# Layer 0: half mean on another engine, tile rounds in another order, virtual-row matmul first in its bank

## The reference

```
# layer 0
g  = groupnorm(x)                        # 8 groups of 2 channels, over H and W
Y  = conv3x3(rfft2(g)) + bias            # complex 3x3 convolution in the frequency domain
x1 = x + irfft2(Y)
# layer 1
out = x1 + mean15x15(groupnorm(x1))      # box mean with zero padding
```

## Time and profile before

| what | value |
|---|---|
| median of 3 runs | 4614.39 us (4611.82 to 4618.62) |
| profiled execution | 4609.17 us, span 4607.4 us |
| PE busy | 4004.6 us, 87% |
| DVE busy | 3595.1 us, 78% |
| POOL busy | 2617.5 us, 57% |
| ACT busy | 2369.4 us, 51% |

### The profile page before, as it was taken

One profiled execution on the slowest core, in us unless ns is written; L12 is line 12 of the kernel. 1 busy time (PEld: TensorE's weight loads), 2 busy tenths in 40 slices (PEclk: granted clock), 3 DMA queues, 4 the chain that ended last, 5 costly groups with the idle time before them and its releaser, 6 DMA issues.

```text
span 4607.4 us, 120149 instructions
## 1 busy us (share of the span) xinstructions
PE 4004.6 (87%) x40080; PEld 2607.0 (57%) x40080; DVE 3595.1 (78%) x6413; ACT 2369.4 (51%) x3744; POOL 2617.5 (57%) x2177
## 2 busy tenths in 40 slices
PE   5299898998989989899898998899988998989988
PEld 1155564556645566455655556555565555655557
DVE  7798875987769877698767987679865888659986
ACT  0177523775247742477315773167722776227752
POOL 4087652875437754477535775267742777418765
PEclk9699998999999999899999999999999999999999
DMA  7311173111731127211371114611155111641114
GB/s 167 119 47 44 40 203 98 46 46 54 205 81 46 46 79 200 60 46 46 98 204 39 44 46 129 176 37 46 38 154 151 42 46 33 177 129 46 46 36 138
DMA packets 221883, 406.04 MB, mean 88 GB/s; under 512 B 96049, under 2 KB 171169, under 8 KB 205217
## 3 DMA queue, kind: packets, MB, share of 16 engines
q1 hardware_dynamic: 221600, 402.52, 32.1%
HBM read 255.55 MB, written 146.80 MB: 87 GB/s over the span
## 4 chain that ended last, share of the span: by engine, by line
PE 45%; DVE 25%; issue 16%; ACT 7%; DMA 3%; DVEq 3%; POOL 1%; SPq 1%; ACTq 1%; POOLq 0%
PE h_ps L609 13%; PE p L535 10%; PE p L462 9%; PE p L635 5%; DVE ob_all L1031 5%; DVE ob_all L1037 4%; DVE img L1046 4%; DVE stat L1049 4%; ACT arena L714 3%; PE h_ps L535 3%; DMA img<-in_x 2%; ACT arena L700 2%; PE h_ps L428 1%; PE p L435 1%; DVE ob_all L893 1%
## 5 line engine op out<-in xcount | busy, mean ns | idle before, releaser
L535 PE MATMUL p<-arena,bd_all 64*64 64x512 f16 x16896 | 1311.5, 380 | 171.6 <-DVE ob_all L1037 88.6
L1165 POOL TENSOR_TENSOR arena<-arena 128x512 f16<-128x512 f32 x512 | 591.7, 1156 | 878.4 <-ACT arena L700 799.4
L535 PEld LDWEIGHTS p<-arena,bd_all 64*64 64x64 f16 x16896 | 611.5, 105 | 642.1 <-issue 491.6
L1223 POOL TENSOR_TENSOR arena<-img 128x512 f32<-128x512 f32 x392 | 497.1, 1269 | 588.0 <-PE h_ps L609 559.5
L428 PE MATMUL h_ps<-hilbert,arena 128*128 128x256 f16 (+1 forms) x6240 | 788.1, 276 | 29.8 <-DVE arena L1004 25.1
L680 ACT ACTIVATE arena<-h_ps 128x512 f16<-128x512 f32 x512 | 305.7, 597 | 965.4 <-PE h_ps L609 732.3
L699 ACT ACTIVATE arena<-img,sc 128x512 f16 (+1 forms) x512 | 439.4, 858 | 625.2 <-PE p L579 419.4
L428 PEld LDWEIGHTS h_ps<-hilbert,arena 128*128 128x128 f16 (+1 forms) x6240 | 614.0, 99 | 171.1 <-issue 35.6
L1174 POOL TENSOR_TENSOR ob_all<-ob_all,img 128x512 f32<-128x512 f32 x512 | 658.6, 1286 | 82.9 <-POOL ob_all L1172 72.8
L1172 POOL TENSOR_TENSOR ob_all<-ob_all 128x512 f32<-128x512 f32 x512 | 656.1, 1281 | 31.1 <-DVE ob_all L1037 31.1
L462 PE MATMUL p<-img,bd_all 128*48 128x512 f32 x1024 | 530.6, 627 | 115.9 <-DMA img<-in_x 79.4
(11 more groups left out here) (154 smaller groups left out, 4561.8 us busy)
## 6 DMA issues: line engine op xcount, KB each, us to landing
img<-in_x SPq DMA_DIRECT2D x256, 512.0 KB, 6.9
out<-ob_all SPq DMA_DIRECT2D x512, 256.0 KB, 3.1
bd_all<-bd_dram SPq DMA_DIRECT2D x512, 192.0 KB, 2.2
wrap_mat<-tab_wrap_h SPq DMA_DIRECT2D x512, 32.0 KB, 2.0
bd_dram<-ob_all SPq DMA_DIRECT2D x16, 768.0 KB, 3.5
arena<-tab_hilbert_kernel SPq DMA_DIRECT2D x8, 256.0 KB, 3.3
hilbert<-tab_hilbert SPq DMA_DIRECT2D x1, 522.0 KB, 3.9
cosw<-tab_cosw SPq DMA_DIRECT2D x1, 320.0 KB, 2.8
```

The source lines that it names most:

```text
L535: m = mm(bank[out_half * HP:(out_half + 1) * HP, :], low(half, 6 * lm + (j if own else j + 1)), (g_part if own else h_part)(half, lp), sta ...
L1165: G.tensor_tensor(gp[s][:, 1, :], g32, gp[s][:, 0, :], ALU.subtract).then_inc(g_split, 1)
```

## The change

Three things are done, all in layer 0:

1. The half mean of a row (two columns) is no longer a DVE instruction in `finish_row`, but two POOL instructions in a new function `mean_half`, called in POOL's slot t for row t-3 after `add_terms` and before the running sum, and for the last three rows after the last `add_terms`.
2. The tile rounds of `mix` fill the base, sine and cosine banks in that order (it was cosine, base, sine). The two waits for DVE's terms stand before round 1 and round 3 (they stood before round 0 and round 1).
3. The virtual-row matmul, which closed the base bank, now opens it, ahead of these waits; in the first row of an image its wait for the virtual row moves with it. What waited for `p0_ready` of a finished row to reuse buffers (ACT twice, SP) now waits for `p2_ready`, which is counted by the last round.

```diff
-                        sp.wait_ge(p0_ready, b * T + i * NG + (PRIMED + s - NG + 1))
+                        sp.wait_ge(p2_ready, b * T + i * NG + (s - NG + 1))
...
-                    pe.wait_ge(t1_done, PRIMED + n)
-                    pe.sem_inc(mix_step, 1)
-                    first_half = [(p1[:], 2)] * 3 + [(p0[s], 0)] * 3 + [(p2[:], 4)] * 3
+                    if first == 0 and s == 0:
+                        pe.wait_ge(v_wrap, b + 1)
+                    if first > 0:
+                        pe.wait_ge(x1_done, PRIMED + n - (NG - 1))
+                    mm(p0[s], wrap_mat[s][:], wrap_row[:], start=True, stop=False, skip_group_check=True)
+                    first_half = [(p0[s], 0)] * 3 + [(p2[:], 4)] * 3 + [(p1[:], 2)] * 3
                     for r in range(10):
                         if r == 1:
+                            pe.wait_ge(t1_done, PRIMED + n)
+                            pe.sem_inc(mix_step, 1)
+                        if r == 3:
                             pe.wait_ge(t2_done, PRIMED + n)
-                            pe.sem_inc(mix_step, 1)
-                        if r == 3 and first > 0:
-                            pe.wait_ge(x1_done, PRIMED + n - (NG - 1))
                             pe.sem_inc(mix_step, 1)
...
-                    if first == 0 and s == 0:
-                        pe.wait_ge(v_wrap, b + 1)
-                    mm(p0[s], wrap_mat[s][:], wrap_row[:], start=False, stop=True, skip_group_check=True).then_inc(p0_ready, 1)
+                    m.then_inc(p2_ready, 1)
...
-                        act.wait_ge(p0_ready, PRIMED + n - (NG - 1))
+                        act.wait_ge(p2_ready, n - (NG - 1))
...
-                        act.wait_ge(p0_ready, PRIMED + n - 1)
+                        act.wait_ge(p2_ready, n - 1)
...
                     V.bn_stats(stat[:, t, :], img[:, t, :]).then_inc(x1_counted, 1)
-                    if first * NG + s >= NG:
-                        dve.wait_ge(x1_whole, n - (NG - 1))
-                    dve.wait_ge(x1_counted, n + 1)
-                    V.scalar_tensor_tensor(half_row[:, s, :], stat[:, t, 1:6:3], -0.5, known[:, t, :],
-                                           ALU.mult, ALU.add).then_inc(half_made, 1)
...
+                def mean_half(n, t, s, first):
+
+                    if first * NG + s >= NG:
+                        pool.wait_ge(x1_whole, n - (NG - 1))
+                    pool.wait_ge(x1_counted, n + 1)
+                    G.tensor_tensor(half_row[:, s, :], stat[:, t, 1:6:3], minus_half[:], ALU.mult).then_inc(half_scaled, 1)
+                    pool.wait_ge(half_scaled, n + 1)
+                    G.tensor_tensor(half_row[:, s, :], half_row[:, s, :], known[:, t, :],
+                                    ALU.add).then_inc(half_made, 1)
...
                     if t >= 1:
                         add_terms(n - 1, i * NG + s - 1, (s - 1) % NG, first - (s < 1))
+                    if t >= 3:
+                        mean_half(n - 3, i * NG + s - 3, (s + 1) % NG, first - (s < 3))
                     if sum_t is not None:
                         presum(b * T + sum_t, sum_t)
...
                 add_terms(b * T + T - 1, T - 1, (T - 1) % NG, T // NG)
+                for t in range(T - 3, T):
+                    mean_half(b * T + t, t, t % NG, T // NG)
```

More of the change, by code:

```diff
@@ L202, in build @@
         half_row = sb("half_row", [P, NG, 2])
+        minus_half = sb("minus_half", [P, 2])
         vmean = sb("vmean", [NV, 2])
@@ L249, in build @@
                                                       sem("x1_done"))
-        x1_counted, half_made, x1_whole, stat_fixed = (sem("x1_counted"), sem("half_made"), sem("x1_whole"),
-                                                       sem("stat_fixed"))
+        x1_counted, half_scaled, half_made, x1_whole, stat_fixed = (sem("x1_counted"), sem("half_scaled"),
+                                                                    sem("half_made"), sem("x1_whole"),
+                                                                    sem("stat_fixed"))
         bias_in, bias_added = sem("bias_in"), sem("bias_added")
@@ L554, in mix @@
                             if r == 6:
-                                pe.wait_ge(p2_half, n + 1)
+                                pe.wait_ge(p1_half, n + 1)
                                 pe.sem_inc(mix_step, 1)
-                            m = half_terms(bank, j, r % 3, 0, r < 6, r >= 6)
+                            m = half_terms(bank, j, r % 3, 0, 3 <= r < 6, r >= 6)
                             if r == 2:
-                                m.then_inc(p1_half, 1)
+                                m.then_inc(p0_half, 1)
                             if r == 5:
-                                m.then_inc(p0_half, 1)
+                                m.then_inc(p2_half, 1)
                             if r == 8:
-                                m.then_inc(p2_ready, 1)
+                                m.then_inc(p1_ready, 1)
                         if r >= 1:
@@ L566, in mix @@
                             if r == 4:
-                                pe.wait_ge(p1_half, n + 1)
+                                pe.wait_ge(p0_half, n + 1)
                                 pe.sem_inc(mix_step, 1)
                             if r == 7:
-                                pe.wait_ge(p0_half, n + 1)
+                                pe.wait_ge(p2_half, n + 1)
                                 pe.sem_inc(mix_step, 1)
@@ L573, in mix @@
                             if r == 3:
-                                m.then_inc(p2_half, 1)
+                                m.then_inc(p1_half, 1)
                             if r == 6:
-                                m.then_inc(p1_ready, 1)
-                    if first == 0 and s == 0:
-                        pe.wait_ge(v_wrap, b + 1)
-                    mm(p0[s], wrap_mat[s][:], wrap_row[:], start=False, stop=True, skip_group_check=True).then_inc(p0_ready, 1)
+                                m.then_inc(p0_ready, 1)
+                    m.then_inc(p2_ready, 1)
                 front(0, 0, 0)
@@ L814, in _ @@
             V.memset(sc[:, 24:25], 1.0 / HB)
+            V.memset(minus_half[:], -0.5)
             V.memset(flat[:, 0:4 * 144], 0.0)
@@ L1077, in layer0 @@
                     finish_row(b * T + t, t, t % NG, T // NG)
-                dve.wait_ge(half_made, (b + 1) * T)
+                dve.wait_ge(x1_counted, (b + 1) * T)
+                dve.wait_ge(half_scaled, (b + 1) * T)
                 V.scalar_tensor_tensor(parity_mean, parity_mean, 0.5, known[:], ALU.mult, ALU.add).then_inc(stat_fixed, 1)
```

## The result

The changed kernel takes 5531.6 us (4 runs, 5529.1 to 5533.1) against 4613.1 us for the kernel before beside it: ratio 1.1988, 95% interval 1.1967 to 1.2009. The forecast was 5508 us. Of all executions in this document one was disturbed, one of the six of e9 (5089.0 us at a granted clock of 0.743), and it is in no ratio. The profiled execution went from 4609.2 to 5533.1 us, its span from 4607.4 to 5531.3.

The account below looks back on a forecast made before the run. It took DVE, the fuller partner of TensorE, to bound the kernel before, and a 7.09 us ACT-POOL circle the changed one. Circle +910 and tail -16 us on 4614.4 us gave 5508 us, range 5350 to 5760.

Parts of the forecast that it names:

- The circle of ACT and POOL: Layer 0 rows: normalise, POOL's slot, half mean and ACT's add wait in a ring, 7.09 us a row, +910 us; 83%.
- The total: Whole kernel: +910 and -16 us make +894 us on the median 4614.4 us, giving 5508 us.
- The small operations: POOL's two 128x2 half-mean instructions: 160 ns each, low end -100 us, high end +320 us in all.
- The estimate of 0.31 us: POOL's half-mean operations priced from the skill page's dispatch figure: sum 137 us higher, 5645 us.
- The start of an image: Row 0's rounds wait for the virtual row, 1.0 us later per image, won back by later rows: net nothing.
- The tail: End of layer 0: last half mean 2 us earlier per image, POOL's last presums covered: -16 us for 8 images.
- What bounds the kernel before: Layer 0 rows: DVE and TensorE hand the row to each other, DVE fuller; slack on ACT and POOL.
- a gain that counts only if nothing else is slower: New tile-round order: TensorE could go at its floor, ACT and SP wait about 0.2 us less.
- Rival 3: Layer 0 rows: no circle, DVE's relief shows and TensorE's floor of 4.45 us decides: -271 us, 4343 us; 3%.
- The clock: TensorE in steady rows drops to 1.2 GHz, likelier 8.2 us a row, 6055 us; 4%.

Follow-up runs that it names:

- e9: The kernel of e6, but in each image's first row the virtual-row matmul and its wait close the base bank as in the kernel before: 4393.0 us, ratio 0.9517.
- e3: The changed kernel, but ACT adds the half mean to row t-4 in slot t instead of t-3: 4410.7 us, ratio 0.9559.
- e4: The changed kernel, but POOL makes the half mean at the start of its slot, ahead of split_g: 4405.9 us, ratio 0.9552.
- e7: The changed kernel with two more, unused 128x2 operations on POOL ahead of the half mean: 5667.6 us, ratio 1.229.
- e8: The changed kernel with the virtual-row matmul given five times instead of once: 5535.7 us, ratio 1.2004.
- e10: The changed kernel, but each image's first row closes its base bank with the virtual-row matmul and its wait as before: 5515.3 us, ratio 1.1947.
- e2: The kernel before with only the half mean moved to POOL, rounds and virtual-row matmul as before: 5514.7 us, ratio 1.1959.
- e5: The kernel before, half mean still on DVE but as two one-column instructions with one SBUF tensor and a per-partition scalar: 4517.4 us, ratio 0.9792.
- e6: The half mean of e5 on DVE together with the changed round order and the virtual-row matmul in front: 4401.8 us, ratio 0.9545.

## Why the prediction was right, step by step

- **The circle of ACT and POOL.** Right. e3 and e4 open it at either end and give back 1121 and 1126 us; e7 shows that POOL's idle time is not free, e8 that TensorE's is. The terms of the sum, from the row above: L702 to L1165 1.63 (forecast 1.69), to L1172 1.12 (1.11), to L1174 1.47 (1.48), to L1196 1.26 (1.24), the pair with its wait 0.56 (0.51), to L725 0.14 (0.20), to L702 0.85 (0.86): 7.03 against 7.09. Eight images give +895 us where +910 was forecast.
- **The total.** Of the 24 us by which 5508 is too low, no term is the cause alone: the circle was put 15 us too long, the start and the tail together 42 us too short. That these offset one another in part is luck.
- **The small operations.** 190 and 195 ns, I took 160 of bounds 50 and 511. The estimate of 0.31 us that I had made of the Trainium skill's dispatch figure (GPSIMD Engine Reference, 3.1 Elementwise) is more than a whole such operation takes here, 0.19 us.
- **The start of an image, put at nothing.** Wrong in size. From the normalise of row 3, N(0), to N(1) it was 77.2 us over the eight images and is 100.4 (+23), N(1) to N(3) gives 5.6 back: +18 us. I had priced the wait, but not that the 36 matmuls behind it run at the lower level of the clock in every image. That is the larger part of the 18 us. The rest, 7 us, stays with the old first row: e10 and e2 take 162.4 and 162.2 us from N(0) to N(3), the kernel before 155.1. Its cause was not tested; the earlier trace rows are from one of three images in which the virtual row is ready 6.0 us after N(0), while in the other five images of the kernel before, and in all of e10 and e2, it is 7.4 to 8.6 us. The Trainium skill (TensorE: Matmul & The Clock Gate, HAM oscillation) describes bursts of matmuls behind a wait that start at the low clock. The trace agrees for the start of an image, with 1.00 before and 0.54 behind a wait of 1.09 us, though the waits in the page's example are longer. I had weighed that rule for the steady rows, where e8 finds 7 us.
- **The tail, -16 us.** Wrong in sign. The last half mean is earlier, 24.1 us after N(60) instead of 24.9, but POOL's last presums now lie under DVE's statistics:

```profile
2009.49 5.33 POOL L1188 TENSOR_TENSOR arena<-arena,img 128x512 f32<-128x512 f32 x4
```

and DVE's first two instructions with two inputs from SBUF stand behind them:

```profile
2012.52 0.98 DVE L919 TENSOR_TENSOR sc<-sc 128x1 f32<-128x1 f32 x1
2013.54 1.30 DVE L920 SCALAR_TENSOR_TENSOR sc<-sc 128x1 f32<-128x1 f32 x1
```

  Before they took 0.16 and 0.22 us:

```profile
1667.68 0.16 DVE L915 TENSOR_TENSOR sc<-sc 128x1 f32<-128x1 f32 x1
1667.88 0.22 DVE L916 SCALAR_TENSOR_TENSOR sc<-sc 128x1 f32<-128x1 f32 x1
```

  That is 1.9 us later and 0.9 earlier, about +8 us in all. I had covered the presums and not what they hold up. Circle, start and tail make 895 + 18 + 8 = 921 of the 924 us of span.
- **What bounds the kernel before: DVE, by its fullness.** Wrong, without harm to the sum, which went by measured periods. Its own row has TensorE busier than DVE, 22.13 against 21.71 us. The bound was a circle over two rows through POOL (e5), with a second one close behind it, which is read from the trace of e5. For the same reason "a gain that counts only if nothing else is slower" undersold the rounds: alone they are worth 3.1%. Rival 3 (4343 us if the circle is open) named the right point, but no kernel reached it: e3, e4 and e6 stop near 4400. Their rows take 4.56 us in the mean, TensorE's own pace of 4.49 us, where I took 4.45, and some slower rows; and they have the longer start.
- **The clock** as a bound of the steady rows: refuted, e8.

## What to carry to other kernels

Before a small step is moved to an engine with idle time, write down, slot by slot, what stands behind its reader and what stands in front of the step itself: if the first feeds the second within one turn of the loop, the lengths of both engines add, and idle time on either is no reserve. The same work one slot earlier, or its reader one slot later, made over 1100 us of difference here. And where two engines look full and the periods alternate, look for a circle over two turns before calling one of them the bound.

## What the runs showed of the hardware

- A DVE instruction on two columns takes as long as POOL's running instruction has left: 160 ns to 1.29 us. In 504 of the 512 uses of L1053 in the kernel before its end lies within 0.03 us of the end of a POOL instruction; the other eight began within 0.01 us of POOL's L1174 and took 0.16 us. So the two engines do not meet only at semaphores. It does so when both of its tensors come from SBUF; L1031, L1037 and L1046, with one input from PSUM, keep their length beside POOL (L1031 469 ns at the median alone, 472 beside it), and so does `tensor_scalar` with a scalar per partition, at 0.21 us (e5). The Trainium skill (SBUF — State Buffer, SBUF: two separate sides) has this as a port pair that is locked for a whole instruction; the trace agrees, 0.98 and 1.30 us against 0.16 and 0.22.
- POOL's operation on two columns takes 0.19 us, two of them without a wait between 0.30 us.
- DVE's rolled loop stands still for 0.46 us once per turn without a wait, seen where DVE is near to being the last one (e5, e6). In e5 the loop's own instructions on DVE's queue stand in this time, 104 times: register operations of 139 ns, a count of 40 and a branch of 56 at the median. They are half of the 0.46 us; the other half is not explained.
